# A two-layer graph network kernel: the first loads of ScalarE's queue move into SyncE's, in another order

## What is computed

```python
h = relu(layernorm(x))
x = x + gat(elu(gat(h, adj, W1, att_src1, att_dst1, b1)), adj, W2, att_src2, att_dst2, b2)
h = relu(layernorm(x))
x = x + relu(masked_attention(h @ Wq, h @ Wk, h @ Wv, adj)) @ Wo

# gat(x, mask, W, a_src, a_dst, b): 4 heads of 128 in the first layer, 1 of 256 in the second
xl   = x @ W
e    = leaky_relu(asrc[:, :, None, :] + adst[:, None, :, :])   # asrc = xl . a_src, adst = xl . a_dst
out  = softmax(where(mask, e, -1e9), axis=1)^T @ xl + b
```

## Time and profile before

| | |
|---|---|
| median of 3 runs | 762.29 us (762.11 to 762.79) |
| profiled execution, its own time | 762.18 us |
| span of its profile | 760.3 us |
| TensorE busy | 715.7 us, 94% |
| VectorE busy | 683.5 us, 90% |
| ScalarE busy | 593.3 us, 78% |
| GpSimd busy | 536.5 us, 71% |
| start of VectorE's first instruction | 8.47 us |

### The profile page before, as it was taken

The page is one execution under the profiler, slowest core; times in us unless marked ns, Lnnn a source line. Parts: engine busy times, 40 slices in busy tenths (PEclk is TensorE's granted clock), DMA queues, the critical chain, the costliest instruction groups (busy, mean ns, idle before and its releaser), DMA issues.

```text
span 760.3 us, 26536 instructions
## 1 busy us (share of the span) xinstructions
PE 715.7 (94%) x8398; PEld 592.9 (78%) x8398; DVE 683.5 (90%) x2017; ACT 593.3 (78%) x1865; POOL 536.5 (71%) x733
## 2 busy tenths in 40 slices
PE   0789999999999999999999999999999999999973
PEld 0477788888888888888888888888888888888852
DVE  5878999999999999999999999999999999999773
ACT  0468888788878888888888888888888888788852
POOL 7458777777677677767776777677777767776551
PEclk9999999999999999999999999999999999999995
DMA  6123466756567865676566566666657667555554
GB/s 204 38 54 67 99 119 110 120 112 125 105 119 114 121 113 116 116 116 114 119 119 111 119 115 122 105 121 117 121 110 120 113 123 109 117 114 91 99 106 103
DMA packets 270423, 84.70 MB, mean 111 GB/s; under 512 B 242896, under 2 KB 269904, under 8 KB 270288
## 3 DMA queue, kind: packets, MB, share of 16 engines
q1 hardware_dynamic: 269856, 82.24, 58.4%
q10 hardware_dynamic: 432, 0.79, 0.4%
HBM read 15.86 MB, written 8.39 MB: 32 GB/s over the span
## 4 chain that ended last, share of the span: by engine, by line
PE 78%; DVE 8%; DMA 4%; ACT 4%; issue 4%; SPq 1%; POOL 1%; DVEq 0%; ACTq 0%; POOLq 0%
PE bank L928 28%; PE bank L954 12%; PE bank L1104 7%; PE bank L1064 6%; PE bank L1083 4%; PE bank L1045 4%; PE bank L1053 3%; PE bank L980 3%; DMA hT<-h_split 3%; ACT e L554 2%; PE bank L1006 2%; PE bank L1004 2%; PE bank L996 2%; PE bank L970 1%; PE bank L969 1%
## 5 line engine op out<-in xcount | busy, mean ns | idle before, releaser
L554 ACT ACTIVATE e<-bank,nmx,q_power 128x128 f32<-128x128 f32 x512 | 194.5, 479 | 5.1 <-DVE nmx L853 4.9
L408 POOL CAST e_split<-e 128x512 f16<-128x512 f32 x128 | 89.7, 701 | 111.1 <-ACT e L554 111.1
L410 POOL TENSOR_TENSOR e_split<-e,e_split 128x512 f16<-128x512 f32 x128 | 152.1, 1188 | 10.3
L954 PE MATMUL bank<-w,h1T 128*128 128x258 f32 x512 | 122.5, 381 | 0.0
L422 POOL TENSOR_TENSOR rstd<-var,minus_half 128x1 f32<-128x1 f32 x128 | 71.7, 560 | 65.6 <-DVE var L718 65.6
L954 PEld LDWEIGHTS bank<-w,h1T 128*128 128x128 f32 x512 | 96.4, 190 | 15.7 <-DVE h1T L749 1.4
L928 PE MATMUL bank<-w_split,hT 128*128 128x260 f16 x768 | 98.0, 278 | 6.1 <-DVE w_split L649 4.9
L505 ACT ACTIVATE eT<-lr,nmx 128x128 f32<-128x128 f32 x256 | 102.6, 455 | 0.8 <-DVE nmx L805 0.8
L928 PE MATMUL bank<-h2T,proj_split 128*128 128x128 f16 x1536 | 96.2, 219 | 1.6 <-DMA h2T<-h_split 1.6
L928 PEld LDWEIGHTS bank<-h2T,proj_split 128*128 128x128 f16 x1536 | 91.0, 98 | 3.5 <-DMA h2T<-h_split 2.1
L928 PEld LDWEIGHTS bank<-w_split,hT 128*128 128x128 f16 x768 | 71.1, 98 | 17.3 <-DVE w_split L649 5.0
(11 more groups left out here) (120 smaller groups left out, 1907.6 us busy)
## 6 DMA issues: line engine op xcount, KB each, us to landing
x_in<-in_x_dram SPq DMA_DIRECT2D x64, 128.0 KB, 2.3
out_dram<-x_out SPq DMA_DIRECT2D x64, 128.0 KB, 2.0
adj_in<-in_adj_dram SPq DMA_DIRECT2D x64, 64.0 KB, 2.4
e3T<-e_split SPq DMA_TRANSPOSE x128, 3.1
hT<-h_split SPq DMA_TRANSPOSE x64, 2.6
h2T<-h_split SPq DMA_TRANSPOSE x64, 2.5
attT<-att_split SPq DMA_TRANSPOSE x64, 2.6
w<-in_L_gnn_W_dram SPq DMA_DIRECT2D x2, 256.0 KB, 6.1
```

The source lines that it names most:

```text
L408: pool.tensor_copy(e3_split[:, g.two, half, 0], e).then_inc(s[high_set], 1)
L410: pool.tensor_tensor(e3_split[:, g.two, half, 1], e, e3_split[:, g.two, half, 0], ALU.subtract).then_inc(s[low_set], 1)
L554: ins = act.activation(e3[:, g.two, h, :], S[:, h // 4, (h % 4) * N:(h % 4 + 1) * N], ACT.Exp, bias=nmx3[:, g.two, h:h + 1], scale=q_power ...
L954: ins = pe.matmul(X2[:, 0:D + 2], h1T[:, g.two, k * F:(k + 1) * F], w2[:, k, :], start=k == 0, stop=k == H - 1)
```

## The change

The two loads of the attention vectors and the load of b1 are taken out of ScalarE's queue and put into SyncE's. SyncE's order is now: W1 in two halves, the two attention vectors of the first layer, x of graph 0, adjacency of graph 0, b1, x of graphs 1 and 2, and then as before. ScalarE issues no DMA any more. No wait, no tile and no computation is changed.

```diff
             for k in range(KD):
                 sp.dma_start(w1[:, k, :, 0:HF // 2], W1[k * 128:(k + 1) * 128, :].rearrange("p (a c) -> p a c", a=2)).then_inc(s["w1_in"], 16)
-            for n in range(3):
+            for k in range(2):
+                sp.dma_start(att1[:, k, :], (att_src1, att_dst1)[k].rearrange("h f -> (h f)").partition_broadcast(128)).then_inc(s["att1_in"], 16)
+            sp.dma_start(x_in[:, 0, :], x[0]).then_inc(x_here[0], 16)
+            sp.dma_start(adj_in[:, 0, :], adj[0]).then_inc(adj_here[0], 16)
+            sp.dma_start(b1_all[:, :], b1.partition_broadcast(128)).then_inc(s["b1_in"], 16)
+            for n in range(1, 3):
                 sp.dma_start(x_in[:, n, :], x[n]).then_inc(x_here[n], 16)
-            sp.dma_start(adj_in[:, 0, :], adj[0]).then_inc(adj_here[0], 16)
...
         @block.scalar
         def _(act):
-            for k in range(2):
-                act.dma_start(att1[:, k, :], (att_src1, att_dst1)[k].rearrange("h f -> (h f)").partition_broadcast(128)).then_inc(s["att1_in"], 16)
-            act.dma_start(b1_all[:, :], b1.partition_broadcast(128)).then_inc(s["b1_in"], 16)
-
```

## The result

| | runs | median us | lowest to highest |
|---|---|---|---|
| before | 22 | 761.98 | 760.17 to 762.79 |
| changed | 22 | 762.93 | 761.80 to 763.86 |

The ratio is 1.0014 with a 95% interval of 1.0008 to 1.0020: 0.95 us slower by the medians. That lies in the range of 760.5 to 763.6 and inside the 0.2% that were taken as no change, but with 22 runs a side the interval leaves no change out. The likeliest case, no shift at all, did not happen; the rival that puts b2 at 15.5 us and costs 1.1 us did.

The account below looks back on a forecast made before the run. TensorE was taken to bound the long middle, so only its start could move, gated by b2 and GpSimd's products. Terms 0 + 0 - 0.1 on the median 762.29 gave 762.2 us, range 760.5 to 763.6.

Parts of the forecast that it names:

- The likeliest case: Start stays gated by b2, landing near 14.4 us; total within 0.4 us of the forecast 762.2; chance 0.50.
- the rival that puts b2 at 15.5 us: Start: SyncE's lone queue moves only 0.20 MB by 5 us; +1.1 us, 763.4; chance 0.10 with late-issue slowdown.
- The bound and the transfer to the end: TensorE bounds the middle, busy 637.75 of 640.00 us; without slack there, a shift of the start reaches the end unchanged.
- Parts 1 and 2: Start: dropping ScalarE's three issues gains 0; SyncE's three extra issues take 1.5 us but are covered, cost 0.
- Part 3: Start, load landings: w1 at 5 to 6 us, attention vectors at 7.7, bounds 6.4 to 8.2.
- Part 4: Start: four products on GpSimd and VectorE take 3.5 us, ending at 11.2 instead of 12.0; VectorE gains 0.8 us.
- Part 5: Start: b2 still lands near 14.4 us, GpSimd's products still end at 19.4, so L645 gains only 0.1 us.
- The lock: Start: short VectorE instructions wait until the GpSimd product under way ends; L609 takes 1.10 us instead of 0.17.
- One of the signs of being wrong: Start: the prediction is wrong if L645 starts before GpSimd's fourth product ends.
- The pace step: TensorE's projection blocks drop from 2.78 to 1.49 us; one block earlier or later moves the end 1.3 us; chance 0.04.
- the issue case: Start: b2 issued 1.5 us later, landing at 15.9; +1.5 us, 763.8; chance 0.10 together with the slow single start.
- The faster rival: Start: without ScalarE's spread vectors both landings come 1.6 us sooner, b2 at 12.8; total 760.7; chance 0.13.

Follow-up runs that it names:

- e4: Kernel before, with GpSimd's four products of the second weight one step later; 760.21 us, ratio 0.9979 to the kernel before.
- e5: Changed kernel, with vector and bias loads reading 128 distinct weight rows instead of one row 128 times; 760.20 us, ratio 0.9986 to the kernel before.
- e6: Kernel before, with vector and bias loads reading 128 distinct weight rows instead of one row 128 times; 760.41 us, ratio 0.9985.
- e3: Changed kernel, with GpSimd's four products of the second weight one step later; 760.87 us, ratio 0.9986 to the kernel before.
- e7: Changed kernel, with the first layer's two attention vectors back in ScalarE's queue, b1 staying in SyncE's; 761.13 us, ratio 0.9999 to the kernel before.
- e10: Changed kernel, measured again unchanged; 762.66 us, ratio 1.0013 to the kernel before.
- e8: Changed kernel, with the two attention vectors back in ScalarE's queue and GpSimd's four products one step later; 760.59 us, ratio 0.9993 to the kernel before.
- e2: Changed kernel, with the second weight, its vectors and b2 loaded behind Wq, Wk, Wv and Wo; 763.53 us, ratio 1.0021 to the kernel before.
- e12: Kernel before with GpSimd's four products one step later, measured again; 759.26 us, ratio 0.9970 to the kernel before.

## Why the prediction was wrong

- **The bound and the transfer to the end**: right in the main. The middle is as busy as before, and most shifts of the start came through (e4: first block 2.2 us ahead, 1.6 us of time by the ratio; changed: third block 0.6 to 1.0, 0.95). That a shift arrives unchanged is not shown: e5 and e6 are 0.7 us apart at the first block and equal in time, and the middle itself differs by up to 1.9 us between two traces of one kernel.
- **Parts 1 and 2, the issues**: right. ScalarE gains nothing. SyncE's first transpose comes at 17.10 against 17.30, and b2 is issued at 7.30 against 7.10, not the 1.5 us later that I summed: issues in SyncE's queue took mostly 0.43 us this time, where the three x loads of the kernel before had taken 2.57 us together.
- **Part 3, the landings**: half wrong. w1 lands at 4.76 (I said 5 to 6). The vectors land at 8.81, outside the bounds of 6.4 to 8.2 and 1.1 us above the value. The bounds treated every megabyte as equal; those 0.52 MB are read from two single rows.
- **Part 4, the products**: the 3.5 us for four products held (3.48). The end at 12.29 instead of 11.2 follows from the landing; the gain of 0.8 us became a loss of 0.3. This may be a second way of the loss beside part 5, since e3 is still 0.66 us behind e4 with the gate away.
- **Part 5, the step that failed**: "b2 still has the same 2.69 MB at or ahead of it in all queues together, so it still lands near 14.4". It landed at 15.55 (in the second pair at 14.88, against 13.76 before). The bytes ahead were the same, so they do not fix the landing. What the runs show in its place: it depends on which queue the two vectors stand in (e7 gave them back to ScalarE's queue, and b2 landed at 7.40 + 5.4 = 12.8) and on how the loads read (e5 took the single row away and got 13.0). Why is open. My reading is that in the kernel before the packets of w1 and x filled the engines beside the slow loads of one row, and that in one queue everything behind them waits; e6, where b2 is 1.9 us sooner than in e5 with no such load in either, says that this is at most a part. The lock, the other half of part 5, worked as told (1.10 us again at L609, the first to fall in e3); it turned the late b2 into 0.6 us. One of the signs of being wrong was badly chosen: L645 did start before the fourth product ended, yet it was held inside its own duration.
- **The pace step**: the prediction read the granted clock as full in the slow block at 29.35. In the changed kernel the window from 29.70 to 32.90 us, over its second block (29.95, 2.78 us again), shows a granted clock of 0.50, and so does that block in e10; the step is one of the clock. It did not move to another block in either pair.
- **The rival that came nearest**, slower by a slow single start, had b2 at 15.5 and 763.4 us. Its place and price were right and its reason was not: the first 5 us were the faster ones (0.66 MB), and the loss came in the next five. I gave it 0.10 with the issue case together, because I took the low GB/s from 2 to 5 us of the earlier trace rows for a slow start of the engines, where much of it was the vectors' load (0.97 MB instead of 0.56 in the first 5 us of e6). That the result lies in the stated range is in this sense luck. The faster rival named that load and then assumed that moving it makes it vanish.

The rule of the Trainium skill cited ahead ("DMA: Bandwidth & Descriptors", "Issuing engines are not separate DMA queues") says that a second issuing engine saves issue time alone. For ordinary rows the times of this case agree (e5 and e6 are equal), and of the 1.9 us between their landings of b2 1.4 are issue time. For loads of one row it does not: e7 and the changed kernel differ in the queue of two such loads, issue b2 at 7.40 and 7.30, and differ in how long it then takes to land (5.4 us, and 6.7 in e8, against 8.2, and 7.6 in e10) and by 0.15% in time. The measurement decides here.

Open: why b2 lands later from one queue; how much of the loss comes by b2 and the gate and how much by the vectors; which part of a load of one row is slow, the reading or something else that depends on the source; and how much of e8's missing gain is chance.

## What to carry to other kernels

An order of need by bytes is not an order of landing: here a load that spreads one row over all partitions held up what stood behind it more than its bytes explain, and it was better in a queue beside others than at the head of the only queue. When a load is made earlier, look at what gates the next step: here VectorE stood still for GpSimd's products, whose start hung on the last and least of the loads, and moving those products by one step was worth more (0.2 to 0.3%) than any order of loads. For effects of a microsecond take several traces and many times: a trace of the fastest or slowest run misleads, and the shift at one point of a single pair can be as large as the effect.

## What was not expected of the hardware

- A stretch of 5 us with loads of one row moved 1.15 MB, with the same loads from distinct rows 1.68 MB, in one queue and with equal sizes.
- VectorE instructions can be held for most of a GpSimd instruction, one after another, and the wait stands in their duration, not in the idle time: 1.10 us in place of 0.17 for L609 on two numbers per partition, and 2.69 in place of 0.92 for the two of L645 in e2.
- The landing of the same load moves between executions by 0.7 us (b2 in two traces of the kernel before) to over 1 us (the vectors, 8.66 to 9.89 in five traces in which SyncE's queue issues them behind w1).
- Spreading two rows of 512 numbers by fp32 matmuls with a row of ones took 3.75 us at the start of the kernel; the products that wait for them started at 9.77 us, against 8.81 with the spread loads.
- The long middle, with TensorE busy over 99% of it, takes up to 1.9 us more or less from one execution of the same kernel to the next (e4 and e12).
